# A fused attention and refinement kernel on one core: stores behind the next pair's transfers, LN1 ahead of the softmax, Pool's passes behind it, a query product ahead of r1

## The reference

```python
# layer 0: attention over channels in 8 heads, then a gated convolution
xn = ln_last(x, ln1_g, ln1_b)                  # LN1, over a row of 32
q, k, v = [conv3x3(conv1x1(xn)) for each].reshape(B, HEADS, HW, d)   # d = 4
probs = softmax(einsum('bhpd,bhpe->bhde', k, q) / scale)
x = conv1x1(einsum('bhpd,bhde->bhpe', v, probs), o_w) + x            # x1
xn = ln_last(x, ln2_g, ln2_b)                  # LN2
gate, info = gelu(conv3x3(conv1x1(xn, g1), g3)), conv3x3(conv1x1(xn, i1), i3)
x = conv1x1(gate * info, r1) + x               # x2
# layer 1: convolution, instance norm, leaky ReLU, then refinement
out = leaky(instance_norm(conv3x3(x, conv1)))
out1, mask = conv3x3(out, conv2), sigmoid(conv3x3(out, mask_w))
xm = out * mask
q, k, v = 1x1 products of xm
attn = softmax over the 9 neighbours of sum_c q * k_shifted
out2 = sum over the 9 neighbours of attn * v_shifted
result = x + out1 * mask + (1 - mask) * out2
```

## Time and profile before

| | us |
|---|---|
| median of 3 runs | 213.72 (213.09 to 216.68) |
| the profiled execution: time | 214.38 |
| its span, first to last instruction | 212.6 |
| around the span | 1.78 |
| TensorE busy (matmul) | 176.6, 83% |
| TensorE weight loads | 117.2, 55% |
| DVE busy | 148.0, 70% |
| ACT busy | 103.8, 49% |
| POOL busy | 62.5, 29% |
| mean granted TensorE clock | 0.949 |

### The profile page before, as it was taken

The page is one execution under the profiler, slowest core; times in us unless marked ns, Lnnn a source line. Parts: engine busy times, 40 slices in busy tenths (PEclk is TensorE's granted clock), DMA queues, the critical chain, the costliest instruction groups (busy, mean ns, idle before and its releaser), DMA issues.

```text
span 212.6 us, 7202 instructions
## 1 busy us (share of the span) xinstructions
PE 176.6 (83%) x3124; PEld 117.2 (55%) x3132; DVE 148.0 (70%) x354; ACT 103.8 (49%) x191; POOL 62.5 (29%) x55
## 2 busy tenths in 40 slices
PE   2599879899997999918996089999779899799991
PEld 2469339387844567715743044677545544566760
DVE  7799599883788676892878715059673785894752
ACT  2168182226648134546568001255851874955850
POOL 7510702800008003910009400072204400460092
PEclk9999999999999999967999755999999999999998
DMA  6514011222010000022000300000001000000002
GB/s 191 95 56 107 2 49 49 62 51 54 2 52 12 14 10 6 3 51 52 0 3 0 109 12 13 0 6 3 12 5 49 20 3 10 15 5 10 3 3 99
DMA packets 12991, 6.91 MB, mean 33 GB/s; under 512 B 10592, under 2 KB 11328, under 8 KB 12960
## 3 DMA queue, kind: packets, MB, share of 16 engines
q1 hardware_dynamic: 12720, 5.88, 10.7%
q10 hardware_dynamic: 240, 0.58, 0.8%
HBM read 3.35 MB, written 1.05 MB: 21 GB/s over the span
## 4 chain that ended last, share of the span: by engine, by line
PE 48%; DVE 19%; issue 14%; POOL 8%; DMA 4%; ACT 4%; SPq 1%; POOLq 1%; DVEq 0%; ACTq 0%
PE ps L1376 10%; PE ps L1475 9%; PE ps L1437 8%; PE ps L1349 5%; DMA w3b<-in_w_gi 3%; POOL ln_s L496 3%; PE ps L1342 2%; PE ps L1334 2%; DVE sh_ln L351 2%; PE ps L1499 2%; DVE gi L1080 2%; DVE ln_out L971 2%; PE ps L1537 1%; DVE sh_in L330 1%; PE ps L1388 1%
## 5 line engine op out<-in xcount | busy, mean ns | idle before, releaser
L496 POOL TENSOR_TENSOR ln_s<-ln_s,neg_half 128x16 f32<-128x16 f32 x7 | 20.8, 2965 | 80.8 <-DVE ln_s L944 80.8
L1437 PE MATMUL ps<-ln_out,w_gi 32*64 32x256 f32 x1152 | 35.4, 384 | 0.4 <-ACT v L643 0.4
L1475 PE MATMUL ps<-sh_in,w_in 96*32 96x256 f32 x384 | 27.1, 437 | 9.4 <-DMA sh_in<-act_c 7.5
L1437 PEld LDWEIGHTS ps<-ln_out,w_gi 32*64 32x64 f32 x1152 | 25.3, 133 | 8.0 <-issue 4.7
L1376 PEld LDWEIGHTS ps<-w_qk,sh_ln 128*128 128x128 f32 x192 | 23.2, 200 | 4.2 <-issue 3.1
L1376 PE MATMUL ps<-w_qk,sh_ln 128*128 128x128 f32 x192 | 24.3, 286 | 0.4 <-DVE sh_ln L351 0.4
L1475 PEld LDWEIGHTS ps<-sh_in,w_in 96*32 96x32 f32 x384 | 13.2, 124 | 20.5 <-issue 12.9
L621 ACT ACTIVATE sh_ln<-ln_out 32x256 f32<-32x256 f32 (+1 forms) x28 | 14.6, 520 | 7.8 <-DVE ln_out L922 4.8
L621 ACT ACTIVATE sh_x<-x 32x496 f32<-32x496 f32 (+1 forms) x20 | 12.3, 617 | 9.5 <-DVE x L1088 6.4
L520 POOL TENSOR_TENSOR res<-out,x 128x512 f32<-128x512 f32 x4 | 5.1, 1280 | 33.4 <-ACT out L691 32.2
L330 DVE COPY sh_in<-act_c 32x496 f32<-32x496 f32 (+1 forms) x28 | 12.8, 458 | 0.5
(11 more groups left out here) (139 smaller groups left out, 327.2 us busy)
## 6 DMA issues: line engine op xcount, KB each, us to landing
sh_ln<-ln_out SPq DMA_DIRECT2D x20, 64.0 KB, 2.1
x_res<-in_x SPq DMA_DIRECT2D x4, 256.0 KB, 2.8
out_x<-out_s SPq DMA_DIRECT2D x4, 256.0 KB, 2.0
x_norm<-in_x SPq DMA_DIRECT2D x3, 256.0 KB, 2.6
kc<-in_shape_consts ACTq DMA_DIRECT2D x1, 450.0 KB, 5.5
w3b<-in_w_gi SPq DMA_DIRECT2D x1, 288.0 KB, 5.7
x_norm<-in_x SPq DMA_DIRECT2D x2, 128.0 KB, 2.8
sh_in<-act_c SPq DMA_DIRECT2D x4, 64.0 KB, 2.0
```

The costliest lines, as they stand in the source:

```text
L496: nc.gpsimd.tensor_tensor(ln_s[n][:, 3, :], ln_s[n][:, 2, :], neg_half[:, :], ALU.pow)\
L1437: mm = nc.tensor.matmul(ps[EC * i:EC * i + EC, r, BLK * m:BLK * m + BLK], w_gi[rows, dx, m, dy, :], src[rows, i, dy:dy + RH, dx:dx + W], s ...
L1475: mm = nc.tensor.matmul(ps[C * r:C * r + C, bank, BLK * i:BLK * i + BLK], w_in[:, i, k, dy, :], plane(sh_in)[:, i, RH * r + dy:RH * r + dy ...
```

## The change

On SP, the store of a pair moves behind the next pair's plane copy and halo, into the next step; in `step(1, False)` the LN2 edges of pair 2 also go ahead of the plane. On DVE, in step 0, `ln_var`, `ln_apply` and `ln1_neighbours` of pair 3 come ahead of `window_softmax`, its plane copies behind `window_probs`; LN2's centre and variance of pair 2 move from step 1 into step 0, around `gated`, and its application to the head of step 1. DVE takes the second half of every pair's `probs_t`, of which ACT keeps the first. On Pool, `residual(0)` waits for LN1 of pair 3, and within every `residual` the second pass waits for the first. On TensorE, the query and key product of pair 3's first image goes ahead of `reduce_1(1)`, in bank 4, and its ACT copy ahead of the x2 planes; the second image and the value product then fill step 1. `mask_conv` does both images in a row with `by_head` behind; the head product of pairs 2 and 3 lies in bank 5, and the wait for `head_max` moves from ahead of `conv2` to ahead of `window_k`. `reduce_1`, `window_scores` and `window_out` wait for halves. Step 1 has six fillers for three; at the start, `v_by_head(1)` goes ahead of `gram(1)` and two fillers fall away.

The diff, without the hunks that only name the new banks:

```diff
@@ -263,8 +263,8 @@
-        g_t_sb = signal("probs_t_in_sbuf", [4] * (PAIRS - 1) + [2], start=1)
-        g_t_dve = signal("last_probs_t_in_sbuf", [0] * (PAIRS - 1) + [2])
+        g_t_sb = signal("probs_t_in_sbuf", 2, start=1)
+        g_t_dve = signal("probs_t_in_sbuf_by_dve", 2, start=1)
@@ -287,6 +287,14 @@
+        def by_head_bank(pair):
...
+            return head_bank(pair) if pair < 2 else 5
...
+        def qk_bank(pair, i):
...
+            return 4 if pair == PAIRS - 1 and i == 0 else i
@@ -444,14 +452,17 @@
                 load_res(pair + 2)
-                in_planes(pair)
-                ln2_edges(pair + 1)
-                halo(pair)
                 if norm:
+                    in_planes(pair)
+                    ln2_edges(pair + 1)
+                    halo(pair)
                     ln1_planes(pair + 3)
                 else:
+                    ln2_edges(pair + 1)
+                    in_planes(pair)
+                    halo(pair)
+                    store(pair - 1)
                     ln2_edges(pair + 2)
-                store(pair)
@@ -469,6 +480,7 @@
             halo(but_last)
+            store(but_last - 1)
             in_planes(last)
@@ -519,6 +531,7 @@
+                pool.wait_ge(g.sem, g.at(pair, 1))
@@ -544,6 +557,7 @@
                     rstd(0, pair + 3)
+                    pool.wait_ge(g_ln[0].sem, g_ln[0].done(pair + 3))
                     residual(pair)
@@ -735,11 +749,9 @@
-                    for h in range(1 if early else 2):
-                        rows = slice(KSLOT * h, KSLOT * h + KSLOT)
-                        nc.scalar.activation(p_t[rows, 4 * R * t:4 * R * t + 4 * R, h, :],
-                                             ps[rows, values_banks(early)[t], :].rearrange("p (q m) -> p q m", m=TH * TW),
-                                             ACT.Copy).then_inc(g_t_sb.sem, 1)
+                    nc.scalar.activation(p_t[0:KSLOT, 4 * R * t:4 * R * t + 4 * R, 0, :],
+                                         ps[0:KSLOT, values_banks(early)[t], :].rearrange("p (q m) -> p q m", m=TH * TW),
+                                         ACT.Copy).then_inc(g_t_sb.sem, 1)
@@ -758,8 +770,9 @@
                 load_exp_table()
-                qk_t_evac(pair + 2, 0)
-                squares(1, pair + 1)
+                if norm:
+                    qk_t_evac(pair + 2, 0)
+                    squares(1, pair + 1)
                 lrelu(pair)
@@ -781,6 +794,9 @@
+                if norm:
+                    squares(1, pair + 2)
+                    qk_t_evac(pair + 3, 0)
@@ -1004,10 +1020,13 @@
+            def ln1_planes(pair):
+                planes("ln1", ln1_out, sh_ln1, g_ln[0], g_v4, pair)
...
-                planes("ln1", ln1_out, sh_ln1, g_ln[0], g_v4, pair)
+                ln1_planes(pair)
@@ -1190,13 +1209,13 @@
-            def last_probs_t(pair):
+            def probs_t(pair, early=False):
...
-                                          ps[KSLOT:P, values_banks(True)[t], :].rearrange("p (q m) -> p q m", m=TH * TW))\
+                                          ps[KSLOT:P, values_banks(early)[t], :].rearrange("p (q m) -> p q m", m=TH * TW))\
@@ -1219,13 +1238,17 @@
                     x1_sum(pair + 1)
-                ln2_center(pair + 1)
-                inorm(pair)
-                ln_var(1, pair + 1)
+                    ln2_center(pair + 1)
+                    inorm(pair)
+                    ln_var(1, pair + 1)
+                else:
+                    ln2_apply(pair + 1)
+                    inorm(pair)
                 inorm_mean(pair)
...
                 in_planes(pair)
-                ln2_apply(pair + 1)
+                if norm:
+                    ln2_apply(pair + 1)
                 head_scores(pair + 2)
@@ -1234,20 +1257,27 @@
                 head_mix(pair + 2)
                 if norm:
                     ln1_center(pair + 3)
+                    ln_var(0, pair + 3)
                 x1_sum(pair + 2)
                 if norm:
-                    ln_var(0, pair + 3)
+                    ln_apply(0, ln1_out, "ln1", pair + 3)
+                    ln1_neighbours(pair + 3)
                 else:
                     ln2_center(pair + 2)
                 window_softmax(pair)
-                if norm:
-                    ln1_apply(pair + 3)
-                else:
+                if not norm:
                     ln_var(1, pair + 2)
                 window_probs(pair)
-                if not norm:
+                if norm:
+                    ln1_planes(pair + 3)
+                    probs_t(pair)
+                    ln2_center(pair + 2)
+                else:
+                    probs_t(pair)
                     ln2_apply(pair + 2)
                 gated(pair + 1)
+                if norm:
+                    ln_var(1, pair + 2)
                 x2_all(pair + 1)
             first_center(0)
@@ -1307,8 +1337,9 @@
             window_softmax(last, True)
+            probs_t(but_last)
             window_probs(last)
-            last_probs_t(last)
+            probs_t(last, True)
             final(last)
@@ -1365,11 +1396,14 @@
-                if pair > 1:
+                if qk_bank(pair, i) == 4:
+                    pe.wait_ge(g_t_sb.sem, g_t_sb.done(pair - 3))
+                    pe.wait_ge(g_t_dve.sem, g_t_dve.done(pair - 3))
+                elif pair > 1:
...
-                        to = ps[:, i, 2 * P * h:2 * P * h + 2 * P]\
+                        to = ps[:, qk_bank(pair, i), 2 * P * h:2 * P * h + 2 * P]\
@@ -1420,7 +1454,6 @@
-                pe.wait_ge(g_score.sem, g_score.at(pair, 3))
@@ -1441,8 +1474,9 @@
-                pe.wait_ge(g_gi.sem, g_gi.done(pair))
...
+                    if r % 2 == 0:
+                        pe.wait_ge(g_gi.sem, g_gi.at(pair, r // 2 + 1))
@@ -1451,6 +1485,9 @@
+                    pe.wait_ge(g_t_dve.sem, g_t_dve.before(pair))
+                    if pair + 2 == PAIRS - 1:
+                        pe.wait_ge(g_qkt_sb.sem, g_qkt_sb.at(pair + 2, 1))
@@ -1524,8 +1561,8 @@
-                pe.wait_ge(g_k_sb.sem, g_k_sb.done(pair))
...
+                    pe.wait_ge(g_k_sb.sem, g_k_sb.done(pair) if bank else g_k_sb.at(pair, 1))
@@ -1552,10 +1589,11 @@
-                pe.wait_ge(g_t_sb.sem, g_t_sb.done(pair))
-                if early:
-                    pe.wait_ge(g_t_dve.sem, g_t_dve.done(pair))
...
+                    half = t // (UNITS // 4)
+                    if t % (UNITS // 4) == 0:
+                        pe.wait_ge(g_t_sb.sem, g_t_sb.at(pair, half + 1))
+                        pe.wait_ge(g_t_dve.sem, g_t_dve.at(pair, half + 1))
@@ -1566,22 +1604,30 @@
             def step(pair, norm):
-                qk(pair + 2, 0)
-                qk(pair + 2, 1, (0,))
+                if norm:
+                    qk(pair + 2, 0)
+                    qk(pair + 2, 1, (0,))
+                else:
+                    qk(pair + 2, 1)
+                    v_by_head(pair + 2, (0,))
                 conv1(pair)
-                qk(pair + 2, 1, (1,))
+                if norm:
+                    qk(pair + 2, 1, (1,))
+                else:
+                    v_by_head(pair + 2, (1,))
                 average_mean(pair)
-                v_by_head(pair + 2, (0,))
+                if norm:
+                    v_by_head(pair + 2, (0,))
                 average_var(pair)
-                v_by_head(pair + 2, (1, 2))
+                v_by_head(pair + 2, (1, 2) if norm else (2,))
                 gram(pair + 2)
-                mask_conv(pair, images=(0,))
+                mask_conv(pair)
                 by_head(pair + 2)
-                mask_conv(pair, images=(1,))
                 front_read(pair + 2)
...
                 gate_info(pair + 1, range(3))
+                pe.wait_ge(g_score.sem, g_score.at(pair + 2, 3))
                 window_k(pair)
@@ -1593,7 +1639,10 @@
                 window_out(pair)
-                stay_busy(3, 6)
+                if norm:
+                    qk(pair + 3, 0)
+                else:
+                    stay_busy(6, 6)
                 reduce_1(pair + 1)
@@ -1612,10 +1661,9 @@
             qk(1, 1)
+            v_by_head(1)
             pe.wait_ge(s_wgi, 3)
             gram(1)
-            v_by_head(1)
-            stay_busy(2, 4)
             pe.wait_ge(s_wready, W_ALL)
@@ -1623,7 +1671,6 @@
             gate_info(0, range(3, 18))
-            pe.wait_ge(g_score.sem, g_score.at(1, 3))
             attn_out(1)
```

More of the change, by code:

```diff
@@ L637, in qk_t_evac @@
                 act.wait_ge(g_gram.sem, g_gram.before(pair))
-                nc.scalar.activation(qk_t[:, i, :], ps[:, i, :], ACT.Copy).then_inc(g_qkt_sb.sem, 1)
+                nc.scalar.activation(qk_t[:, i, :], ps[:, qk_bank(pair, i), :], ACT.Copy).then_inc(g_qkt_sb.sem, 1)
             def v4_evac(pair):
@@ L1029, in head_max @@
                 dve.wait_ge(g_rep.sem, g_rep.done(pair))
-                nc.vector.tensor_scalar(sm[:, 0, :], ps[:, head_bank(pair), 2 * P:2 * P + 2 * D], inv_scale[:, 0:1], None,
```

(3 more changed lines are left out.)

## The result

The changed kernel takes 197.86 us (median of four executions, 197.17 to 198.72) against 213.8 for the kernel before: ratio 0.927, 95% interval 0.920 to 0.933. Repeated later, on two chips, it gave 0.923 (0.918 to 0.928) and 0.920 (0.915 to 0.924). The forecast was 197.0 with 193.5 to 203.

The account below looks back on a forecast made before the run. The prediction saw TensorE held up by pair 1's plane, queued behind a store, and by DVE's late probabilities of pair 0. Its terms summed to -17.1 us, giving 197.3 or 196.6; it forecast 197.0 us, range 193.5 to 203.

Parts of the forecast that it names:

- Start and masks of pair 0: Up to window_q of pair 0: earlier fillers and reduction give -0.4, head product behind both images gives -0.5 us.
- Pair 0's back end: Window_q of pair 0 to conv1 of pair 1: LN1 ahead of the softmax, probabilities sooner; -4.2 us, bounds -5.9 to -1.2.
- The collision that I took at nothing: Pair 0's back end: Pool's passes against a multiplication of the probabilities on DVE; +1.1 us by the rule, none taken.
- what I priced at nothing: Conv1 to masks of pair 1: Pool's final passes of pair 0 meet DVE's scaling; tanh comes only three microseconds later.
- Conv1 to masks: Conv1 to masks of pair 1: DVE's copies, not the plane's DMA, release the masks after 9.4 us; -7.2 us.
- Masks to window_q: Pair 1's masks to window_q: 5.8 us instead of 10.49 if the remaining hole doesn't lower the clock; -4.6, or 0.
- the rival: Clock rival: the hole ahead of pair 1's masks lowers the clock; price 4.6 us, time 201.6, chance 0.13.
- Pair 1's back end and tail: After window_q of pair 1: back end +0.3 us from fillers, tail -0.5 as window scores wait for half the keys.
- the back end as long as before: Rival: pair 0's back end stays as long, LN1 only changing place; price 4.2 us, time 201.2, chance 0.11.
- The shared port: Rival: Pool's passes beside softmax and probabilities cost 3.0 us, as they cost LN1; time 200.0, chance 0.08.
- The late plane: Rival: pair 1's plane stays late, queued on SP behind the LN2 edges; gain only 5.3 us, about 208.5, chance 0.04.
- slower: Rival: clock falls at pair 0's transposes or pair 1's masks, low up to pair 1's window_out; 219 us, chance 0.02.

Follow-up runs that it names:

- The run with the buffer: Changed kernel with a buffer of its own for the residual's product, so the second Pool pass doesn't wait for the first: 196.73 us, 0.917.

## Why the prediction was right

*Start and masks of pair 0 (-0.4, -0.5).* -1.19 in the profile, but 0.83 of it was there already when pair 1's query and key product started (31.11 for 31.94), before any edit acts. From there to conv1 of pair 0 it takes 26.48 or 26.49 us in the three profiles without the edits of the start and 26.08 to 26.12 in the eleven with them: -0.4, as forecast. The masks gave -0.52.

*Pair 0's back end (-4.2; -4.56).* Step by step on the new clock, 1.71 earlier: LN1 2.25 for 2.3; the softmax's end 85.16 for 85.4; the probabilities' end 88.78 for 88.5. The collision that I took at nothing came: Pool's passes lasted 1.35 a piece with their gaps and the last lay under the first half's multiplication, +0.63 and not +1.1. My own times had it, for by them that multiplication starts at 88.0 and the passes end at 88.5; I looked at the second half's alone. It cost nothing on the path, since ACT, copying LN1 planes until 90.84, was later than the transposes, which ended at 89.55: window_out starts at 91.51, released by ACT's p_t, as I had it. The product ahead of r1 took 2.94 for 2.9, and r1 to conv1 4.77 for 4.81. The gating ended at 95.36, only 0.1 ahead of r1 and not 0.9, the collision's 0.63 being most of the difference; that the cover was still enough is luck. DVE and TensorE are both at the edge here. Undoing LN1's move (+5.5) and the product's (+3.4), each by itself, costs 8.9 together, more than the 6.2 us that all edits but the stores, LN2 and the head product gave (204.06 to 197.88). That suggests that each pays only beside the other; part of both costs is the low clock behind the new waits, and no run takes out both.

The Trainium skill's page "SBUF — State Buffer", section "Who interferes with whom", nearly fits the multiplication: it started 0.49 into Pool's pass and ended 0.51 after it, where the full block that this section states would leave all of its 0.66 for after; the reduction beside the same pass kept 0.64. And it bears on what I priced at nothing: this section of the Trainium skill counts a scaling by a tensor_scalar among those that can contend, when its operands allow it, and beside Pool's final passes that scaling took 2.01 us, where it took 0.61 in the run with the stores alone. It cost nothing here, for it ended at 112.37 and the masks' tanh came at 114.66.

*Conv1 to masks (-7.2; -7.22).* 9.35 for 9.4, released by DVE's copies; the plane, issued at 105.92, waits for nothing. Undoing the order alone brings back the wait for the plane (8.27 us in that profile).

*Masks to window_q (-4.6; -2.52 or -4.71).* The one mis-sized term, and only in the executions with the lower clock. I had taken it as all or nothing and the hole ahead of the masks as the cause. The low clock came, but it held only for the first half of the masks, at 2.2 us in this profile and not 4.6, and it came before that hole, under pair 3's scores. So the rival is half right, and what lowers the clock stays open. Where the clock stays up, the term is right to 0.1.

*Pair 1's back end and tail (+0.3, -0.5; together +0.21).* The back end is +0.40. In the tail the scores wait 0.61 for 1.04 as forecast, but Pool's extra wait in the residual, which I took at 0.1, shifts a pass into DVE's scaling (2.17 for 1.68), and the tail gives -0.19. The run with the buffer shows that this wait was worth 0.7.

Of the rivals, the back end as long as before is what the run with all of LN1 in its old place shows (33.67), and is averted by the change. The shared port beside the softmax and the probabilities cost 0.63 in all, not 3.0, and the softmax lost nothing where the passes ran beside it (LN1's application behind the softmax). Beside LN1, where Pool's wait keeps the passes away, it costs 2.4 (the run without that wait). The late plane didn't come, for the LN2 edges were issued at 101.41, well ahead of it. In the rival *slower* the working slips: losing 21.4 us at 0.8 on each microsecond takes some 27 us of slowed work and not 21. In the profile of after the low clock lasted 6.5.

## What to carry to other kernels

Price a moved step with the engine that runs beside it in view: the early place of LN1's application was worth nothing until Pool was made to wait for it, and the early variance, which let Pool's passes out of the way, 3.8 us by itself. An edit that removes one wait shows its worth only with those that keep the next work from filling the hole: the stores alone gave 5.9 us, with LN2 and the head product 10.8. A product that stands ahead of a critical step may be free, if another engine holds that step up anyway.

## What the runs showed of the hardware

The granted clock isn't a function of the program alone. With the same work and the same waits (0.30 and 0.96 us for the averages, 1.0 to 1.6 ahead of pair 1's masks) it stayed at 1.00 in two profiles of the changed kernel. In the profile of after it fell to 0.50 between 107.0 and 107.5, under pair 3's scores and ahead of the last wait; in the run with the residual's buffer it fell between 111 and 112, in the midst of the first image's masks, which ran from 109.89. Both times TensorE was busy when it fell. Of 22 executions of the changed kernel and of the one with the residual's buffer, 6 had a mean clock near 0.98; of the 12 with idle matmuls in these waits, none. That suggests that the fillers prevent it, and it isn't enough to show it.

Part of the spread comes from the first 31 us. Conv1 of pair 0 started at 57.93, 58.40 and 59.01 in three profiles at the full clock with the same instructions ahead of it, and the spans, 195.3, 195.8 and 196.4, follow it: from there to the end all three take 137.4. The differences arise ahead of pair 1's query and key product, where the loads of inputs and weights stand; which of the waits there makes them isn't shown.
